# Second normalise ahead of the inverse deviation, and the second norm's transposes and router between the groups of heads

## The reference

```
x = x + xattn(layernorm(x), ctx)      # q, k, v, out with low-rank additions
x = x + moe(layernorm(x))             # top 2 of x @ gate_w, softmax over the 2
```

## Time and profile before

| | |
|---|---|
| median of 3 runs | 750.47 us (748.65 to 753.04) |
| profiled execution | 753.71 us, of which the span 751.9 us |
| mean granted clock of TensorE | 0.975 |
| busy, share of the span | PE 90%, DVE 73%, POOL 66%, ACT 61% |
| one pass of the loop | 26.2 us, PE 25.24 us busy |

### The profile page before, as it was taken

One profiled execution on the slowest core, in us unless ns is written; L12 is line 12 of the kernel. 1 busy time (PEld: TensorE's weight loads), 2 busy tenths in 40 slices (PEclk: granted clock), 3 DMA queues, 4 the chain that ended last, 5 costly groups with the idle time before them and its releaser, 6 DMA issues.

```text
span 751.9 us, 22958 instructions
## 1 busy us (share of the span) xinstructions
PE 675.2 (90%) x7980; PEld 563.7 (75%) x7981; DVE 546.3 (73%) x1239; ACT 455.2 (61%) x770; POOL 494.8 (66%) x582
## 2 busy tenths in 40 slices
PE   6637799999999999999999999679999979999994
PEld 2226688788788878888887888568878868988983
DVE  3853779898999889899998988845746545555552
ACT  1435878777777877787788778524543424434441
POOL 3124655887887788788778878735776536655665
PEclk9998999999999999999999999889999989999998
DMA  9911101201212121121112111123566665544550
GB/s 262 314 54 44 29 25 34 77 30 45 75 45 61 45 75 36 44 71 46 59 45 75 38 52 61 44 73 80 87 109 96 94 167 99 83 69 80 93 77 1
DMA packets 51557, 56.31 MB, mean 75 GB/s; under 512 B 15105, under 2 KB 45825, under 8 KB 51521
## 3 DMA queue, kind: packets, MB, share of 16 engines
q1 hardware_dynamic: 37136, 38.50, 18.1%
q0 software_dynamic: 14384, 17.33, 13.6%
HBM read 30.67 MB, written 25.76 MB: 75 GB/s over the span
## 4 chain that ended last, share of the span: by engine, by line
PE 44%; POOL 16%; issue 13%; DVE 12%; SPq 4%; ACT 4%; DMA 3%; another core or an unknown queue 1%; POOLq 1%; DVEq 0%; ACTq 0%
PE ps L1513 29%; POOL prob L894 6%; PE ps L1621 5%; POOL prob L887 4%; PE ps L1631 4%; DVE picked L1406 3%; DVE mx L1316 3%; POOL rows_dram L941 2%; PE ps L1686 2%; PE ps L521 2%; POOL out_x L491 2%; DVE ot_s L1253 2%; POOL ln_s L904 1%; ACT ot_s L1045 1%; DMA pt_s<-in_wo 1%
## 5 line engine op out<-in xcount | busy, mean ns | idle before, releaser
L491 POOL DMA_INDIRECT out_x<-pt_s,token_of x78 | 125.3, 1607 | 30.8 <-issue 30.3
L580 ACT ACTIVATE q_s<-ps 128x512 f32<-128x512 f32 x78 | 46.5, 596 | 124.3 <-PE ps L1513 114.0
L708 DVE TENSOR_TENSOR wq_s<-q_s,wq_s 128x512 f16<-128x512 f32 x78 | 55.5, 714 | 86.7 <-ACT wq_s L584 77.1
L1513 PE MATMUL ps<-q_s,ffnw 128*128 128x256 f16 x936 | 113.0, 279 | 1.6 <-issue 1.5
L1513 PE MATMUL ps<-ffnw,wq_s 128*128 x936 | 109.4, 273 | 3.5 <-issue 3.3
L1513 PEld LDWEIGHTS ps<-ffnw,wq_s 128*128 128x128 f16 x936 | 89.7, 98 | 19.2 <-issue 8.1
L1513 PEld LDWEIGHTS ps<-q_s,ffnw 128*128 x936 | 91.7, 100 | 14.9 <-issue 2.6
L887 POOL TENSOR_TENSOR prob<-prob,mx 128x1168 f32<-128x1168 f32 x64 | 77.8, 1237 | 37.9 <-DVE mx L1316 37.9
L1513 PE MATMUL ps<-wo_s,ot_s 128*128 128x256 f16 x768 | 89.4, 273 | 5.4 <-DVE ot_s L1253 5.4
L1513 PE MATMUL ps<-xt_s,wq_s 128*128 128x256 f16 x768 | 90.1, 279 | 2.2 <-DVE xt_s L1253 1.9
L1513 PEld LDWEIGHTS ps<-xt_s,wq_s 128*128 128x128 f16 x768 | 76.6, 100 | 13.4 <-issue 1.9
(11 more groups left out here) (210 smaller groups left out, 1236.8 us busy)
## 6 DMA issues: line engine op xcount, KB each, us to landing
prob<-rows_dram SPq DMA_DIRECT2D x39, 264.0 KB
wstage<-in_ffn_w SPq DMA_DIRECT2D x16, 512.0 KB, 3.6
x_sb<-in_x SPq DMA_DIRECT2D x4, 1024.0 KB, 11.1
out_x<-x_sb SPq DMA_DIRECT2D x16, 256.0 KB
rows_dram<-wstage SPq DMA_DIRECT2D x8, 264.0 KB
out_x<-pt_s,token_of POOLq DMA_INDIRECT x78
pt_s<-in_wq SPq DMA_DIRECT2D x2, 512.0 KB, 4.4
pt_s<-in_wo SPq DMA_DIRECT2D x2, 512.0 KB, 8.7
```

The source lines that it names most:

```text
L491: pool.indirect_dma_start(out_rows, bass.IndirectOffsetOnAxis(ap=token_of[:, j % UNROLL, c:c + 1], axis=0), y_sb[:, j % UNROLL, c, :], Non ...
L580: act.activation(h32[:, half, :], h_ps(t, j, half), ACT.Silu, scale=1 / WSCALE).then_inc(silu_done, 1)
L708: dve.tensor_tensor(hs[:, j % 2, 1, 2 * half:2 * half + 2, :].rearrange("p f n -> p (f n)"), h32[:, half, :], hs[:, j % 2, 0, 2 * half:2 * ...
L1513: last = pe.matmul(o, lhs(a, n), rhs(c, n), start=(i == 0), stop=(i == len(steps) - 1))
```

## The change

Four edits in the bodies. On GpSimd the second normalise goes ahead of `rstd_2` in all but the last body, where it was so already. The odd keys go to bank 3 instead of 1 from the second batch on, and `new_keys` waits for `slots` instead of the first value split. `transpose_2(b - 1)` goes from between the sixth and the seventh transposes of probabilities to between groups 0 and 1 of the heads, and `router(b - 1)` from between groups 0 and 1 to between 1 and 2; on ScalarE the norm goes behind the sixth high half and the router's copy behind the heads' first. The heads use banks 4 to 7 in order.

```
             return ps[:, (5, 1)[k] if isinstance(b, int) and b == 0 else (0, 3)[k], :]    # was: else k
...
             return ps[:, 4 + k, :]                                                        # was: (4, 6, 5, 7)[k]
...
                 normalise(b, 0)
                 if routed and not last:
                     scatter(b - 2, 0)
-                if not first and not last:
+                normalise(b, 1)
+                if not first:
                     rstd_2(b - 1)
-                normalise(b, 1)
                 if last:
-                    rstd_2(b - 1)
                     scatter(b - 2, 0)
...
                 pt(b, 1)
-                if not first and not last:
-                    normalise_2(b - 1)
                 pt(b, 2)
...
                 pt(b, 4)
-                if last:
+                pt(b, 5)
+                if not first:
                     normalise_2(b - 1)
-                pt(b, 5)
-                if not first and not last:
-                    x2t_copy(b - 1)
                 pt(b, 6)
                 pt(b, 7)
                 ot(b, 0)
+                if not first and not last:
+                    x2t_copy(b - 1)
                 ot(b, 1)
...
                     pe.wait_ge(q_split, 4 * b + 8)
-                    pe.wait_ge(v_split, 2 * b + 1)
+                    if not first:
+                        pe.wait_ge(slots, b)
                     new_keys(b + 1)
...
                 transpose_probs(b, 5)
-                if not first and not last:
-                    pe.wait_ge(pt_split, 8 * b + 2)
-                    transpose_2(b - 1)
...
                 for k in range(4):
                     pe.wait_ge(pt_split, 8 * b + 5 + k)
                     if k == 1 and not first and not last:
-                        pe.wait_ge(slots, b)
+                        transpose_2(b - 1)
+                    if k == 2 and not first and not last:
+                        pe.wait_ge(k_split, 2 * b + 4)
                         router(b - 1)
                     attend(b, k)
```

More of the change, by code:

```diff
@@ L360, in keys_bank @@
         def keys_bank(k, b):
-            return ps[:, (5, 1)[k] if isinstance(b, int) and b == 0 else k, :]
+            return ps[:, (5, 1)[k] if isinstance(b, int) and b == 0 else (0, 3)[k], :]
         def values_bank(k):
@@ L387, in heads_bank @@
         def heads_bank(k):
-            return ps[:, (4, 6, 5, 7)[k], :]
+            return ps[:, 4 + k, :]
         x_bank, out_bank = (ps[:, n, :] for n in (4, 5))
```

## The result

The changed kernel takes 756.31 us (752.63 to 761.11, 20 runs), the kernel before 750.05 in the same session; the ratio is 1.0085, 95% interval 1.0068 to 1.0102. That is 6.3 us slower. The forecast was +2.9 us (753.4), with a range of 748.5 to 757.5. So the sign and the range held, but the time lies where the rival "the router's wait is longer" stood, and the chances had put more on "same" than on "slower".

The account below looks back on a forecast made before the run. TensorE was taken as the bound, waiting 0.53 us for GpSimd's late second normalise, with a VectorE loop almost as long. 13 passes at +0.19 and batch 1 at +0.39 gave +2.9 us, 753.4; range 748.5 to 757.5.

Parts of the forecast that it names:

- the router's wait is longer: Rival: the router's copy on ScalarE comes later than summed, each tenth lost reaching the projection; 754.3 to 757.5 us; chance 0.33.
- GpSimd no longer late, VectorE next: Second half's transposes start 0.8 us earlier, but VectorE's split stays at 326.39, so group 0 gains only 0.19.
- Odd keys: Bank 3 spares the key products their 0.29 us wait for the first value split; they end 0.3 earlier.
- Transposes and router between the groups: Group 0 to projection becomes 6.02 us, router waiting for its ScalarE copy; projection 333.23 against 333.04, pass 0.19 longer.
- No DMA moves: With the inverse deviation behind the second normalise on GpSimd, the second pair of scatters still starts at 325.1.
- The sum: 13 loop passes at +0.19 give 2.5 us; with batch 1 and the last batch, together +2.9 us.
- Batch 1: Heads not late there before; the stretch from group 0 to projection becomes 6.02 for 5.63 us, so +0.39.
- Last body: The last batch only swaps one split and the norm on ScalarE: zero, at most 0.5 us either way.
- The crowd on ScalarE: Longer-wait rival's reason: group 0's copy, the norm's two halves and three splits stand ahead of the router's copy on ScalarE.
- The hidden wait: Rival: router's wait is covered, group 0 to projection takes 5.65 to 5.9 us; 748.0 to 751.5; hidden or cancelled 0.10.
- VectorE not the floor: Rival: VectorE's splits follow the earlier transposes, a pass changes by -0.4 us, total near 745; chance 0.06.
- The product (L1403) did get longer: Rival: GpSimd's later subtraction holds VectorE's product longer, second query group late, +0.4 us a pass, some 756.5; chance 0.03.

Follow-up runs that it names:

- kernel 1: Changed kernel with the second norm's transposes ahead of head group 0 and the router's copy ahead of group 0's on ScalarE: 741.33 us, ratio 0.9902, pass 25.63.
- kernels 2: Changed kernel with ScalarE copying the second norm's transposes, for the router, ahead of head group 0: 751.91 us, ratio 1.0045, pass 26.29.
- kernel 4: Changed kernel with the second scatters moved behind GpSimd's next subtraction and ScalarE's row copy behind the last group's copy: 752.23 us, ratio 1.0041, pass 26.30.
- kernel 9: Changed kernel with the router's copy ahead of group 0's on ScalarE, and the second scatters and row copy later: 750.52 us, ratio 1.0017, pass 26.30.
- kernel 5: Changed kernel with only ScalarE's row copy moved behind the last group's copy, scatters left in place: 757.39 us, ratio 1.0109, pass 26.49.
- kernel 10: Changed kernel with transposes ahead of group 0, router's copy first, and the second scatters and row copy later: 745.43 us, ratio 0.9948, pass 25.84.

## Why the prediction was right in sign and too small in size

*GpSimd no longer late, VectorE next.* Right, though GpSimd is 0.31 us later than forecast: the second normalise ends at 303.64, 324.01 on the ruler (forecast 323.70). The first subtraction starts 289.69 - 286.45 = 3.24 us into the pass, before it was 309.75 - 306.82 = 2.93; the forecast had this 0.3 from the later scores but didn't carry it on to the normalise and the scatters. Still, the second half's transposes wait for nobody. VectorE's split starts at 305.92, 326.29 on the ruler, 0.10 ahead of its old place, and TensorE waits for it ahead of group 0, as forecast. Group 0 starts 0.73 after that split began, not 0.82. So group 0 came at 327.02 and not at 327.21: 0.38 us were gained up to there, not 0.19. It is the first of the two mis-sized terms, and a favourable one.

*Odd keys.* The wait was read as 0.29 us. It was worth more: the keys' first product starts 302.17 - 286.45 = 15.72 us into the pass, before it was 322.99 - 306.82 = 16.17, 0.45 earlier. A run of matmuls that need not wait begins before the modelled end of the run ahead of it, so the idle time shown ahead of a wait is less than what the wait costs. In the changed kernel VectorE's split lets no more than the 0.38 us through to group 0; in kernel 1 the bank alone is worth 0.47 a pass.

*Transposes and router between the groups.* This is the step that failed in size. The forecast let ScalarE take up group 0 after 0.84 + 0.04 = 0.88 us; it took 1.27 (307.92 - 306.65). Everything behind it followed as worked out, only later: the router's copy 0.50 behind group 0's, the router 0.14 behind the copy's end. From group 0 to the projection the forecast had 6.02 us; it became 6.38. "No DMA moves" failed with it: the second pair of scatters starts at 305.06, 325.43 on the ruler, not 325.1, and its last DMA ends at 307.39, 0.11 ahead of group 0's end. Whether a pair left at 325.1 would have spared the wait no run shows. Where the pick-up is prompt the term was nearly exact. Batch 1, which has no scatters, shows it:

```profile
121.34 0.85 PE L1628 MATMUL ps<-pt_s,v_s 128*64 128x256 f16 x12 [0.39 <-DVE pt_s L1250]
...
123.55 1.03 PE L1683 MATMUL ps<-gate_f,x2t 128*128 128x8 f32 x8
...
127.43 0.28 PE L1510 MATMUL ps<-wo_s,ot_s 128*128 128x256 f16 x1
```

127.43 - 121.34 = 6.09, and no wait is shown ahead of the router. Two passes of the loop are like that as well, the first and the last: there the copy starts 0.04 after group 0's end (147.63 + 0.85 = 148.48, copy at 148.52), and the first takes 153.72 - 127.43 = 26.29 us, as in kernels 2, 4 and 9.

*The sum.* Forecast per pass -0.19 + 0.38 = +0.19; in the pass shown -0.38 + 0.74 = +0.36, over all 13 passes +0.28. Two errors, of 0.19 and 0.36 us, had opposite signs; that they partly cancelled is luck. Batch 1: +0.45 for +0.39. Last body: +0.30 for 0, inside the 0.5 allowed. The 1.8 us outside the bodies weren't in the sum, and remain open.

*The rivals.* The longer wait of the router, with a chance of 0.33, came true in its place and its price: group 0's copy stands ahead of the router's, and what is lost there, 0.39 us on the pick-up (1.27 for 0.88), goes to the projection. The crowd on ScalarE that it gave as the reason did not: ScalarE stood idle for 0.45 us ahead of group 0's copy, and kernels 4 and 5 show the scatter as the cause. The hidden wait is out: no pass of the changed loop is under 26.29, and from group 0 to the projection it is at least 6.09, not 5.65 to 5.9. "VectorE not the floor" is out for the changed kernel, which waits 0.30 us for VectorE. The product (L1403) did get longer, 2.14 us with the subtraction starting 0.07 ahead of it, against 1.84; it used up a part of VectorE's idle time (0.44 us left of 0.62) and stayed off the path. That the product was held at all, with the subtraction first, agrees with the rule of the Trainium skill, "SBUF — State Buffer", section "Who interferes with whom". Kernel 4 puts the product first in 6 of its 13 passes, kernel 9 in 6 and kernel 10 in 12, by 0.02 to 0.04 us, and it then takes 0.18 us, as the rule has it (kernel 4, VectorE and GpSimd):

```profile
283.31 0.18 DVE L1403 TENSOR_TENSOR picked<-picks,place 128x32 f32<-128x32 f16 x1
```

```profile
283.33 2.44 POOL L887 TENSOR_TENSOR prob<-prob,mx 128x1168 f32<-128x1168 f32 x2
```

That pass takes 26.29 us, and so does the one ahead of it, in which the subtraction is first and the product takes 2.16: the hold is off the path there.

*What the forecast didn't ask.* It priced the four edits as one path and never each against the other loop. The runs show that the edits have no prices of their own to add up: the GpSimd order and the bank bring 0.7 us a pass in the changed kernel and 1.2 in kernel 1, beside a move that costs 1.0 without them. No run has them without the move, and none changes the heads' banks by themselves.

## What to carry to other kernels

When a wait that one engine causes is removed, ask which work was lying under it for free, and put that work under the wait that comes next: the transposes cost some 0.6 us of the path behind VectorE's split and next to nothing ahead of it, and that move, with the router's copy put ahead of group 0's, turned a change that is 0.85% slower into one that is 1.0% faster. If a result has to go over another engine and back, give it a whole stretch of other work as cover, and put its copy first in that engine's queue. An idle time shown ahead of a matmul understates how much earlier it could start, since without the wait it would have started inside its predecessors' modelled end (0.29 shown, 0.45 gained at the keys); how much of that reaches the end of the pass depends on the next wait.

## What was not expected of the hardware

A result of TensorE that ends beside GpSimd's second indirect DMA of a pair can reach ScalarE late: by 0.42 us in the changed kernel and 0.38 in kernel 5, where it ends some 0.1 behind that DMA, and by 0.77, 1.17 and 1.37 in kernels 4, 9 and 10, where it ends while that DMA runs. Other results in the rows above are taken up 0.03 or 0.04 us after their end, also one that ends while the first DMA of the pair runs (kernel 4, 301.05, with the first at 300.34 to 301.38). In one pass of kernel 10 a group that ends 0.23 us ahead of the second DMA's start is late too (427.87, 428.10, taken up at 429.51).

The delay moves with the scatter. In the changed kernel the copy starts 0.53 us after the scatter's end (307.39), in kernels 4, 5, 9 and 10 0.51, 0.46, 0.47 and 0.47 after it (302.66, 303.18, 305.44, 299.84). That it comes from the scatter is shown by kernels 4 and 5; how is open, since the first and the last pass of the changed loop have the same scatter at the same place and no delay.
